# Final stage of a Mamba-2 + mixture-of-experts kernel: second expert rows gathered with addition, x1 added batch by batch, the last batch normalised by two engines and stored in halves

## The reference

```python
x = _layernorm(x + attn(x))                 # x1
x = _layernorm(x + ffn(x))                  # this end
# ffn: logits = x @ gate_w + gate_b; weights, indices = top_k(logits, 2); weights = softmax(weights)
#      out_e = (silu(gh) * xh) @ w2 + b2 for every expert; sum over the two chosen of weight * out_e
# _layernorm: (x - mean) / sqrt(var + 1e-5), over the 256 features
```

## Time and profile before

| what | value |
|---|---|
| time, median of 3 runs | 1474.63 us (1473.24 to 1475.08) |
| the profiled execution: its own time | 1472.57 us |
| its span, first to last instruction | 1470.7 us |
| busy: PE / DVE / ACT / POOL | 88% / 74% / 54% / 55% of the span |
| POOL's first gather of the final stage | at 1346.74 us |
| DVE's first batch of the final stage | at 1435.68 us |

### The profile page before, as it was taken

The page is one execution under the profiler, slowest core; times in us unless marked ns, Lnnn a source line. Parts: engine busy times, 40 slices in busy tenths (PEclk is TensorE's granted clock), DMA queues, the critical chain, the costliest instruction groups (busy, mean ns, idle before and its releaser), DMA issues.

```text
span 1470.7 us, 40051 instructions
## 1 busy us (share of the span) xinstructions
PE 1297.4 (88%) x13108; PEld 1028.9 (70%) x13109; DVE 1087.3 (74%) x2499; ACT 791.8 (54%) x1814; POOL 807.9 (55%) x740
## 2 busy tenths in 40 slices
PE   3889999999999998999872899999999999999970
PEld 1456666656666666666651799999999999999970
DVE  5889999999998898888876566565666565565537
ACT  4656666666666576656540444445444444444434
POOL 2466776766675787677874246060346061052771
PEclk9999999999999998999975899999999999999985
DMA  5203443323343323322512431303030303102594
GB/s 185 98 29 116 130 129 108 97 91 118 103 130 116 108 85 112 115 76 83 180 40 97 148 116 32 118 29 116 31 118 29 121 29 114 36 29 64 136 203 146
DMA packets 94653, 145.70 MB, mean 99 GB/s; under 512 B 13488, under 2 KB 77488, under 8 KB 94448
## 3 DMA queue, kind: packets, MB, share of 16 engines
q1 hardware_dynamic: 79216, 97.06, 20.7%
q0 software_dynamic: 15072, 46.51, 10.6%
q10 hardware_dynamic: 288, 1.19, 0.2%
HBM read 103.06 MB, written 41.67 MB: 98 GB/s over the span
## 4 chain that ended last, share of the span: by engine, by line
PE 60%; DVE 15%; issue 10%; POOL 8%; ACT 3%; SPq 2%; DMA 2%; DVEq 0%; ACTq 0%; POOLq 0%
PE pe L998 13%; PE pa L998 13%; PE py L1010 12%; PE pa L620 4%; PE py L720 3%; POOL arena L2230 3%; DVE arena L1508 3%; PE pa L612 3%; PE pm L756 3%; PE pz L709 2%; PE pt L738 2%; DVE arena L1547 2%; DVE arena L1574 1%; DVE arena L1522 1%; POOL arena L2220 1%
## 5 line engine op out<-in xcount | busy, mean ns | idle before, releaser
L998 PE MATMUL pe<-arena 128*128 128x128 f16 x3408 | 218.5, 220 | 22.5 <-issue 22.5
L998 PEld LDWEIGHTS pe<-arena 128*128 128x128 f16 x3408 | 202.4, 98 | 28.2 <-issue 27.4
L998 PE MATMUL pa<-arena 128*128 128x128 f16 x3408 | 216.1, 219 | 0.0
L1404 ACT ACTIVATE arena<-pe,arena 128x128 f32<-128x128 f32 x568 | 162.2, 372 | 85.1 <-PE pe L998 84.9
L998 PEld LDWEIGHTS pa<-arena 128*128 128x128 f16 x3408 | 198.7, 97 | 0.0
L1010 PE MATMUL py<-arena 128*128 x1704 | 197.6, 273 | 0.8 <-DVE arena L2008 0.8
L1508 DVE SCALAR_TENSOR_TENSOR arena<-pa,arena 128x511 f32<-128x511 f32 (+2 forms) x240 | 178.6, 745 | 7.5 <-ACT arena L1073 1.1
L1980 DVE SCALAR_TENSOR_TENSOR pm<-pa,arena 128x128 f32<-128x128 f32 x284 | 80.6, 352 | 138.1 <-ACT arena L1404 122.6
L1010 PEld LDWEIGHTS py<-arena 128*128 128x128 f16 x1704 | 163.6, 98 | 18.8 <-issue 1.1
L720 PEld LDWEIGHTS py<-arena 128*128 128x128 f32 x1024 | 129.8, 204 | 35.4 <-issue 22.9
L2133 POOL TENSOR_SCALAR arena<-arena 128x1536 f16<-128x1536 f32 (+2 forms) x35 | 42.7, 1220 | 201.8 <-DVE arena L2008 196.8
(11 more groups left out here) (225 smaller groups left out, 2532.5 us busy)
## 6 DMA issues: line engine op xcount, KB each, us to landing
arena<-step_rows SPq DMA_DIRECT2D x64, 512.0 KB, 6.4
arena<-in_w_exp POOLq DMA_DIRECT2D x32, 768.0 KB
arena<-queue SPq DMA_DIRECT2D x74, 129.5 KB, 2.1
answer<-arena SPq DMA_DIRECT2D x71, 128.0 KB, 1.7
arena<-in_x SPq DMA_DIRECT2D x16, 512.0 KB, 6.6
answer<-zeros SPq DMA_DIRECT2D x10, 512.0 KB, 4.7
arena<-h SPq DMA_DIRECT2D x9, 512.0 KB, 6.2
h<-arena SPq DMA_DIRECT2D x8, 512.0 KB, 3.0
```

The lines of the kernel that those rows point to most:

```text
L998: ins = pe.matmul(bank[:, f * P:(f + 1) * P], w_split[:, p, hl, d * 2 * FF + col:d * 2 * FF + col + P], x[:, r, d, :], start=(n == 0), sto ...
L1404: ins = e.activation(sg[:, half, f, :], GATE[half][:, f * P:(f + 1) * P], ACT.Silu, bias=b1a[:, bass.ds(ex_, 1), ff], scale=1.0 / S1)
```

## The change

- The buffer `high` is gone. The higher rows are gathered straight into `total`, by indirect DMAs that add (`compute_op=ALU.add`). DVE's addition and its semaphore go.
- x1 is added per batch: behind the lower gathers of batch b come the four of batch b + 1, then the adding DMA of batch b, which waits for that batch's gathers alone. The higher gathers of a batch wait for that batch's x1.
- The last batch is normalised by two engines: ACT does its first two token tiles, DVE the other two (`tensor_scalar`, two operations with a scalar per partition), and SP stores it as two DMAs of 256 KB.

```diff
-        x1_back = sem("x1_back")
-        f_sum = sem("f_sum")
+        x1_back = [sem(f"x1_back{b}") for b in range(NB)]
...
+            def rows_away(first, end_):
+                sp.dma_start(out[first * P:end_ * P, :].rearrange("(k p) d -> p k d", p=P),
+                             total[:, first:end_]).then_inc(out_done, 16)
-            for b in range(NB):
+            for b in range(NB - 1):
                 sp.wait_ge(f_out, b + 1)
...
+                rows_away(b * NK, (b + 1) * NK)
+            sp.wait_ge(f_half, 1)
+            rows_away(NTILE - HALF, NTILE)
+            sp.wait_ge(f_out, NB)
+            rows_away(NTILE - LG, NTILE - HALF)
...
-                for k in range(LG):
+                for k in range(LG if b < NB - 1 else LG - HALF):
                     row = total[:, b * LG + k]
...
             def spread_of(b):
-                if b == 0:
-                    dve.wait_ge(x1_back, 16 * NB)
                 dve.wait_ge(got[b], 16 * LG)
-                rows_b = total[:, b * LG:(b + 1) * LG, :]
-                dve.tensor_tensor(rows_b, rows_b, high[:, b * LG:(b + 1) * LG, :], ALU.add).then_inc(f_sum, 1)
-                dve.wait_ge(f_sum, b + 1)
                 for k in range(LG):
...
             scale_of(NB - 1)
+            dve.wait_ge(f_scale, NB)
+            for k in range(LG - HALF, LG):
+                row = total[:, NTILE - LG + k]
+                ins = dve.tensor_scalar(row, row, frs[:, NB - 1, k:k + 1], fnb[:, NB - 1, k:k + 1], ALU.mult, ALU.add)
+            ins.then_inc(f_half, 1)
...
+            def add_x1(b):
+                pool.wait_ge(low_got[b], 16 * LG)
+                pool.dma_start(total[:, b * NK:(b + 1) * NK], x1_rows[b * T:(b + 1) * T, :].rearrange(
+                    "(k p) d -> p k d", p=P), accum_op=ALU.add).then_inc(x1_back[b], 16)
+
+            def add_high(b):
+                pool.wait_ge(x1_back[b], 16)
+                for t in range(b * LG, (b + 1) * LG):
+                    pool.indirect_dma_start(total[:, t, :], None, answer,
+                                            bass.IndirectOffsetOnAxis(ap=slot_lh[:, 1, t:t + 1], axis=0),
+                                            compute_op=ALU.add).then_inc(got[b], 16)
...
-            for t in range(NTILE):
-                get_rows(total, t, 0, low_got)
+            get_low(0)
+            for b in range(1, NB):
+                get_low(b)
+                add_x1(b - 1)
+            add_x1(NB - 1)
```

More of the change, by code:

```diff
@@ L52 @@
 LG = NK
+HALF = LG // 2
 CLEAR_STEPS = 10
@@ L299, in build @@
         cmp7, cmpj = carve(NB, NTILE), carve(NB, NJ)
-        high = carve(NTILE, D)
         pa = [ctx.enter_context(nc.psum_tensor(f"pa{i}", [P, T], F32)) for i in range(2)]
@@ L410, in build @@
         slots_ready = sem("slots_ready")
-        low_got = sem("low_got")
+        low_got = [sem(f"low_got{b}") for b in range(NB)]
+        f_half = sem("f_half")
         out_done = sem("out_done")
@@ L562, in _ @@
                 swap_rows(NGRP, r)
-            for b in range(NB):
+            def rows_away(first, end_):
+                sp.dma_start(out[first * P:end_ * P, :].rearrange("(k p) d -> p k d", p=P),
+                             total[:, first:end_]).then_inc(out_done, 16)
+            for b in range(NB - 1):
                 sp.wait_ge(f_out, b + 1)
-                sp.dma_start(out[b * T:(b + 1) * T, :].rearrange("(k p) d -> p k d", p=P),
-                             total[:, b * NK:(b + 1) * NK]).then_inc(out_done, 16)
-            sp.wait_ge(out_done, 16 * NB)
+                rows_away(b * NK, (b + 1) * NK)
[3 more added lines that the diff above has]
+            rows_away(NTILE - LG, NTILE - HALF)
+            sp.wait_ge(out_done, 16 * (NB + 1))
         @block.tensor
@@ L2411, in _, with get_low @@
                 split(e)
[L2414 to L2417, removed]
+            def get_low(b):
+                for t in range(b * LG, (b + 1) * LG):
+                    pool.indirect_dma_start(total[:, t, :], None, answer,
+                                            bass.IndirectOffsetOnAxis(ap=slot_lh[:, 0, t:t + 1], axis=0)
+                                            ).then_inc(low_got[b], 16)
+            def add_x1(b):
[4 more added lines that the diff above has]
+                pool.wait_ge(x1_back[b], 16)
+                for t in range(b * LG, (b + 1) * LG):
+                    pool.indirect_dma_start(total[:, t, :], None, answer,
+                                            bass.IndirectOffsetOnAxis(ap=slot_lh[:, 1, t:t + 1], axis=0),
+                                            compute_op=ALU.add).then_inc(got[b], 16)
             def wait_tiles(s, tiles):
@@ L2432, in _ @@
                     wait_tiles(s, pool.value_load(need_i[0:1, b * WB + s:b * WB + s + 1], min_val=1, max_val=NJ // WB))
[L2433 to L2439, removed]
+                add_high(b)
 def kernel(**inputs):
```

## The result

| | changed kernel | kernel before |
|---|---|---|
| time, median of 18 runs each (lowest to highest), us | 1481.31 (1475.55 to 1486.6) | 1473.97 (1471.46 to 1479.46) |
| ratio, with 95% interval | 1.0044 (1.0032 to 1.0055) | |
| profiled execution: its time, its span, us | 1481.56, 1479.8 | 1472.57, 1470.7 |

The forecast was 1456.2 us, within 1453 to 1466. The change is slower, and the measured median lies 25.1 us above the forecast.

The account below looks back on a forecast made before the run. DVE was taken to bound the kernel, starting late, with POOL close behind. After the change POOL completes the last batch at 1443.1, plus 9.2 gives 1452.3, 18.4 under the span; off the median: 1456.2 us, range 1453 to 1466.

Parts of the forecast that it names:

- from there to the first higher gather: POOL's lower gathers and x1 additions, 50.7 us, plus 1.1 waiting for the last addition and a 0.3 gap.
- 32 higher gathers on POOL: POOL issues the adding gathers at 1.253 us each, the last one done at 1438.9.
- landing, with the stores' excess: Behind POOL's last gather: 3.2 us until it lands, plus 1 for output stores sharing the DMA engines.
- last statistics to the end: The tail after DVE's last statistics, normalising and storing: 9.2 us in place of 9.7.
- I take no difference: An adding gather costs POOL the same 1.253 us as a plain one.
- the upper bound of +0.37: The most an adding gather could cost POOL beyond a plain one, in us; time then 1468.0.
- the rival's own break-even: Rival of a dearer adding gather on POOL, chance 0.11 (1460 to 1471 us): +0.58 us a gather cancels the gain.
- gathers over 1.4 us apart: A sign on POOL that the forecast is wrong; if right, higher gathers come at 1.25 us each.
- DVE's start: DVE begins its batches at 1425.5, with 3.5 us of the earlier 13.7 us hold-up of tiles remaining.
- DVE stays the limit: Rival: tiles still held up by PE's gaps, DVE starts 1428 to 1435.7; time 1457 to 1464.7 us, chance 0.23.
- the halves' worth: Last batch normalised by ACT and DVE, stored as two DMAs: saves 0.5 us, bounds 0 and 1.0.
- row loads late in every tile: Rival: SP's row loads take 8.5 us each beside x1 additions, 31 us lost, time 1482 us; chance 0.05.

Follow-up runs that it names:

- the last experiment: The second experiment's kernel with POOL's `need_i` loads for batch 0 and that batch's higher gathers ahead of the last x1 addition: 1463.8 us, ratio 0.9916.
- the second experiment: The changed kernel with the buffer `high` and DVE's addition back, x1 still spread, last batch still in halves: 1465.51 us, ratio 0.9942 to the kernel before.

## Why the prediction was wrong, step by step

Measured from the first lower gather, which was itself 3.3 us later in this execution (1350.03) than in the profiled one of before, ahead of anything that the change touches (over the ten traces of this document it lies between 1342.55 and 1356.32):

| step of the forecast | forecast | measured | difference |
|---|---|---|---|
| first lower gather | 1346.74 | 1350.03 | +3.3 |
| from there to the first higher gather | 52.06 | 58.01 | +5.95 |
| 32 higher gathers on POOL | 40.1 | 59.0 | **+18.9** |
| landing, with the stores' excess | 4.2 | 3.4 | -0.8 |
| last statistics to the end | 9.2 | 9.35 | +0.15 |
| end of the span | 1452.3 | 1479.8 | +27.5 |

**The step that failed** is "I take no difference" for an adding gather on POOL, and with it the upper bound of +0.37. The mechanism was right: POOL sets the last statistics, through the pitch of its gathers. The term 32 x 1.253 was mis-sized by 32 x 0.60 = 19 us. At +0.58 a gather, the rival's own break-even, the gain is gone, and it measured +0.60. The forecast's own sign of being wrong, gathers over 1.4 us apart, is what came. The estimate was too low because I compared an x1 addition of 512 rows with a plain weight DMA of 128 descriptors and put the difference down to descriptors. Two things differed in that pair, and I chose the wrong one: the same x1 DMA without addition takes 0.76 us, so 0.56 of its 1.32 was the addition, and only 0.76 - 0.55 = 0.21 the other 384 descriptors. The 0.56 stood in the trace of before all along, but no pair of rows there isolates it. And the bound of +0.37 took the 1.32 of an x1 addition as the most that an adding gather could take; it took 1.54, since the addition comes on top of the gather's own 0.95. The whole difference of that pair, 1.32 - 0.55 = 0.77, left as it is and not made smaller for fewer rows, would have put the upper end at 1456.2 + 32 x 0.77 = 1480.8, past no change.

**To the first higher gather, +5.95.** Seven x1 additions between gathers came 6.64 us apart instead of 6.33 ((1399.75 - 1359.89) / 6): an addition between gathers takes 1.46, not the 1.32 of the block, and the gather behind it 1.07; +1.7 in all. The last addition waited 1.53 instead of about 1.1, +0.56 with the longer addition ahead of it. The other 3.7 is a wait that I had not priced at all. In the kernel before, POOL's three register loads of `need_i` for batch 0 began at 1371.7 to 1373.1 and took 0.29 us each: POOL's instruction stream was ahead of its gathers, the last of which began at 1385.73, and the gathers covered them. In the changed kernel they stand behind the wait for the last lower gathers (`low_got7`), so that the stream reached them only at 1402.72, with one addition left to cover them, and there they were slow. The chain of the changed kernel there:

```profile
1402.72 1.32 POOLq L2455
...
1404.56 0.56 POOLq L2455
...
1405.54 1.38 POOLq L2455
...
1407.27 0.77 issue
1408.04 1.45 POOL arena L2435
```

Three loads of 1.32, 0.56 and 1.38 us, where the median of this line is 0.30. That place of the order stands ahead of the prediction, and I had read it for the additions alone. In the last experiment's kernel, which moves these loads, the gap is gone. What makes a load slow can be read from the loads for later batches (durations in ns: least, median, most), in the kernel before while the x1 additions were landing, and with x1 stored plain while that block was:

```profile
L2432 POOLq TENSOR_LOAD <-arena x9: 1053/1345/1748, 1394.4 to 1412.9; - x9
```

```profile
L2432 POOLq TENSOR_LOAD <-arena x12: 284/290/305, 1403.5 to 1417.0; - x12
```

The loads were slow beside x1 transfers that add, and not beside plain ones of the same size.

**What was right.** DVE's start: 78.1 us behind the first gather, forecast 78.8. The batches on DVE: 2.32 us, forecast 2.27. The other five kernels with x1 spread have DVE's start at 77.0 to 80.2, so that was no luck of one execution. The row loads: at most 5.6 us behind single additions, forecast 5.0. The rival "DVE stays the limit" fell, since DVE waits for POOL. Its reason, that PE's gaps belong to the loop's exit, is not settled: they shrank here (0.70 and 1.84 us), but one of 2.66 came back in the last experiment, with x1 spread. The tail was 9.35 us, forecast 9.2; the halves' worth was 0.37, forecast 0.5. The rival "row loads late in every tile" didn't happen. The latest row loads took 5.6, 8.5 and 8.8 us, against a median of 2.1. The Trainium skill (DMA: Bandwidth & Descriptors, "Queues, rings and completion order") says that a DMA engine takes turns between queues at packet boundaries. A row load that is hardly late, as the prediction drew from it, is not what these numbers show.

So the change has two parts of opposite sign. Spreading x1 with the halves, as the second experiment has it, gives 0.58%, 8 us: DVE starts 11.9 us earlier, and waits 3.2 us for gathers later on. The adding gathers turn this into a loss of 0.44%, by about 15 us: they take 1.22 us a batch off DVE, which in the second experiment kept about even with POOL, and put 4 x 0.6 = 2.4 us a batch on POOL, which sets the end. A single adding DMA for the four token tiles of a batch wasn't tried, and neither was a mixture in which only some of the batches add. Why the addition costs POOL this time stays open; the runs show that it is paid per DMA and hardly per row.

## What to carry to other kernels

An addition inside a DMA is not free on the queue that issues it: here it cost POOL 0.52 to 0.6 us a DMA, almost whatever its size. So 32 small ones on the queue that sets the end did not pay; a few large ones, on a queue with time to spare, are what the numbers speak for, and that was not tried. When a price must come from a pair of rows that differ in two things, let the range hold both readings. When an order is changed, also look at what small waits and register loads lose their cover at the seam. Spreading a large block of adding transfers between other work brought DVE's start 11 us forward here.

## What the runs showed of the hardware

- Issue of a DMA on POOL, plain against adding: 0.76 and 1.32 us (direct, 512 rows), 0.95 and 1.54 us (indirect, 128 rows), 0.90 and 1.42 us (indirect, 64 rows).
- A POOL gather that begins during a DVE addition with both inputs in the on-chip memory ends 0.81 or 0.82 us behind the addition's end: the gather's busy time rises from 0.95 to as much as 1.93 us.
- A register load on POOL, with a median of 0.30 us, took 1.05 to 1.75 us while the block of x1 additions was landing in the kernel before, and at most 0.31 while a plain block of the same size was.
- A row load of 129.5 KB on SP's queue took up to 8.5 and 8.8 us beside a block of eight 512 KB transfers on POOL's, adding or plain, and up to 5.6 (5.9 with the plain gathers of 64 rows) with the same transfers spread between gathers, against a median of 2.1.
